# Spectra of 57 complex numbers stored without padding to 64, in a four-layer convolution kernel

## The chip, the cores and the metric

The kernel runs on one core of a Trainium2 chip. That core has a matrix engine (TensorE, PE in the profile), three engines for elementwise work and reductions (VectorE or DVE, ScalarE or ACT, GpSimd or POOL), a queue engine (SyncE or SP) and 16 DMA engines that move data between the chip's DRAM and the on-chip memory of 128 partitions. The metric is the device time of one execution in microseconds (us); each number is a median of runs.

## What is computed

The input x has shape 32 x 64 x 112 x 112, float32. Four residual layers follow each other, each on the group-normalized input (32 groups of two channels):

```
# layer 0: 3x3 convolution of the signs with ternary weights
x = x + conv(sign(gn(x)), round(tanh(w0))) * alpha
# layer 1: spectral mixing
x_ft = rfft2(gn(x), norm='ortho')                      # 112 x 57 complex
xt   = x_ft[:, :, :56, :57]                            # min(64, 112//2), min(64, 57)
out  = einsum('bchw,cohw->bohw', xt, complex(w1))      # w1: 64 x 64 x 64 x 64 x 2
x = x + irfft2(out placed in zeros, s=(112, 112))
# layer 2: 7x7 convolution with bias
x = x + conv(gn(x), w2) + bias
# layer 3: windowed linear attention, windows of 8 x 8
x = x + attention(gn(x))
```

What matters here is layer 1: per image and channel a spectrum of 56 x 57 complex numbers. A row of it, 57 complex numbers, is 114 floats, 456 B.

## The kernel before

There are three stages, each a function with a block per engine. Within a stage every engine runs its own program, written out by hand, and semaphores alone order them. Nothing is scheduled by a planner.

**Stage A, `local_conv_and_forward_dft`** runs over the 32 images. SyncE loads x into `xc` (two halves of 1568 KB). TensorE does the 3x3 convolution from signs, VectorE adds (L316) and writes `x1s`, GpSimd's queue stores it to the DRAM tensor x1 in two halves (`store_x1`, L236). SyncE loads x1 again with image rows in the partitions (`xh`, `turn`, L206), which waits for both halves of the store (L200). TensorE transforms along rows (L470) and along columns (L477); ScalarE puts the results into `freq` (L409), 28 rows per partition, and GpSimd's queue stores them to the DRAM tensor `xf` in two parts of 16 and 12 rows (`store_freq`, L246). GpSimd's queue has, per image, in this order: x1 half 0, xf part 0, x1 half 1, xf part 1.

**Stage B, `mix_frequencies`** runs over KP = 28 steps k, each with two frequency rows at a time. SyncE loads, per pair of steps, weights `wt` (two transfers of 4096 KB, L529) and for each step the spectra `xs` of all images (2048 KB, L537). There are two weight buffers and one `xs`. VectorE turns `xs` into `xt` (L611 to L613), TensorE multiplies (L638), ScalarE and VectorE copy the sums into `ys` (L600, L617), and GpSimd's queue stores them to the DRAM tensor `yf` in four transfers of 512 KB per step (L563). `load_x(k)` waits until step k - 1 was turned (L536).

**Stage C, `large_conv_and_attention`** first prepares weights and then runs over the images: it loads both halves of an image's mixed spectrum into `ys` (`load_ys`, L1000) and x1 into `xr` (L1003), transforms back in two products (L1110 with `ys` as the weights, L1127), and does layers 2 and 3. `ys` is cleared once at the start (L1723). The load of the next image's `ys` is issued when L1110 is done with this one's.

The row length in all transfers comes from one constant:

```
KW = W // 2 + 1        # 57
FR = 2 * KW            # 114 floats of a row that are used
FP = 128               # floats of a row that are stored
```

`freq` has FP floats per row, xf is (KP, P, B, FP), `xs` is [P, B, FP // 2, 2], stage B's `ys` is [P, C, FP // 2], yf is (B, 2, KH, C, FP // 2), and stage C's `ys` is [P, C, FP // 2]. The pads of `freq` and of both `ys` are set to zero once. In stage C only the first 57 of the 64 columns matter: `inv_w` is zero for the others.

Of the kernel before, what the change touches and what calls it, by code (L numbers as in the profile page):

```python
# [14 lines left out]
P = 128  # L15
C = 64
# [5 lines left out]
KH = H // 2  # L22
KW = W // 2 + 1
KP = KH // 2
FR = 2 * KW
FP = 128
ROWS = 4
CHUNKS = J // ROWS
N4 = ROWS * W
# [4 lines left out]
def above_zero(count):  # L34


    return not isinstance(count, int) or count > 0
# [47 lines left out]
def pairs(eng, images, step):  # L85


    if images > 2:
        step(0)
    if images > 4:  # L90
        with eng.Fori(1, images // 2 - 1) as t:
            step(t)
# [30 lines left out]
def local_conv_and_forward_dft(nc, B, x, weight, alpha, cst, x1, xf):  # L123

    with ExitStack() as ctx:
# [7 lines left out]
        yw = sb("yw", [P, 2, KH, C])  # L133
        freq = sb("freq", [P, KP, FP])
        wraw = sb("wraw", [C, C, 9])
# [362 lines left out]
def mix_frequencies(nc, B, weight, xf, yf):  # L498

    with ExitStack() as ctx:  # L500
        sb = lambda name, shape, dt=F32: ctx.enter_context(nc.sbuf_tensor("b_" + name, shape, dt))
        sem = lambda name: ctx.enter_context(nc.semaphore("b_" + name))
        ps = ctx.enter_context(nc.psum_tensor("b_ps", [P, 8, BANK], F32))
        wt = sb("wt", [P, 2, C, 2, FP // 2, 2])
        xs = sb("xs", [P, B, FP // 2, 2])
        xt = sb("xt", [P, 2, KW, 3, B])
        ys = sb("ys", [P, C, FP // 2])
        w_loaded = [sem("w_loaded0"), sem("w_loaded1")]
# [390 lines left out]
def large_conv_and_attention(nc, B, args, cst, x1, yf, out):  # L899

    with ExitStack() as keep:
        sb = lambda name, shape, dt=F32: keep.enter_context(nc.sbuf_tensor("c_" + name, shape, dt))
# [3 lines left out]
        inv_h = sb("inv_h", [P, 2, H])  # L906
# [15 lines left out]
        sem = lambda name: keep.enter_context(nc.semaphore("c_" + name))  # L922
        ps = keep.enter_context(nc.psum_tensor("c_ps", [P, 8, BANK], F32))
        xr = sb("xr", [P, 2, J, W])
        ys = sb("ys", [P, C, FP // 2])


        xp_all = sb("xp", [P, 2 * 9 * (RING + 3) * PW], F16)
# [35 lines left out]
        s = type("Semaphores", (), {n: sem(n) for n in names})  # L964
# [27 lines left out]
        @block.sync  # L992
        def _(sp):
            def load_ys(n):
                if above_zero(16 * n):
                    sp.wait_ge(s.c1_done, 16 * n)
                    sp.nop(nofuse=True)
                for r in range(2):
                    src = yf[bass.ds(n, 1), r].rearrange("b k o w -> (b k) o w")
                    sp.dma_start(ys[64 * r:64 * r + KH], src).then_inc(s.ys_in, 16)  # L1000

            def load_x1(n, odd, a):
                sp.dma_start(xr[:, odd, 8 * a:8 * a + 8],  # L1003
                             x1[bass.ds(n, 1)].rearrange("b hp c j w -> (b hp c) j w")[:, 8 * a:8 * a + 8]
                             ).then_inc((x1_in if a < A7 - 1 else x1_end)[odd], 16)

            def load_next(t, odd, a):
                p = (odd + a) % 2
                sp.wait_ge(out_done[p], (A7 * t + ((A7 * odd + a - p) // 2 + 1)) * 32)
                sp.nop(nofuse=True)  # L1010
                load_x1(2 * t + (2 + odd), odd, a)

            def store(t, odd, more):
                n = 2 * t + odd
                for a in range(A7):
                    sp.wait_ge(s.xo_done, n * A7 + (a + 1))
                    sp.nop(nofuse=True)
                    for hp in range(2):
                        dst = out[bass.ds(n, 1), :, 16 * a:16 * a + 16].rearrange(
                            "b c (j hp) w -> hp (b c) j w", hp=2)[hp]  # L1020
                        sp.dma_start(dst, xr[C * hp:C * hp + C, odd, 8 * a:8 * a + 8]).then_inc(out_done[(odd + a) % 2], 16)
                    if more and a:
                        load_next(t, odd, a - 1)
                if more:
                    load_next(t, odd, A7 - 1)

            sp.wait_ge(s.zeros, 1)
            load_ys(0)
            for a in range(A7):
                load_x1(0, 0, a)  # L1030
            load_ys(1)
            for a in range(A7):
                load_x1(1, 1, a)

            def step(t):
                for odd in range(2):
                    load_ys(2 * t + (2 + odd))
                    store(t, odd, True)

            pairs(sp, B, step)  # L1040
            store(B // 2 - 1, 0, False)
            store(B // 2 - 1, 1, False)
            for p in range(2):
                sp.wait_ge(out_done[p], B // 2 * (A7 * 32))

        @block.tensor
        def _(pe):
# [37 lines left out]
            def stats(count, which):  # L1085
                pe.wait_ge(s.stats_done, count + 1)
                if above_zero(count):
                    pe.wait_ge(s.rstd_done, count)
                pe.matmul(ps[:, STAT_BANK[which], 0:2], group[:], st[:], start=True, stop=True).then_inc(s.grouped, 1)

            def bring(n, odd):
                row = (n - 1) * A7
                if above_zero(row):
                    numerator(row - 1)
                pe.wait_ge(s.ys_in, 32 * (n + 1))
                if above_zero(n):
                    pe.wait_ge(s.t_taken, n * (A7 * NT))
                for g in range(16):
                    if above_zero(row):
                        if g == 8:  # L1100
                            turn_back(row - 1)
                        if g == 12:
                            give_back(row - 1)

                    if g >= 4:
                        pe.wait_ge(s.c1_taken, n * 16 + (g - 3))
                        pe.nop(nofuse=True)
                    for o in range(4 * g, 4 * g + 4):
                        for r in range(2):
                            ins = pe.matmul(ps[64 * r:64 * r + 64, CONV_BANKS[g % 4], H * (o % 4):H * (o % 4) + H],  # L1110
                                            ys[0:120, o], inv_h[0:120, r],
                                            start=(o % 4 == 0), stop=(o % 4 == 3), skip_group_check=True)
                    ins.then_inc(s.c1_done, 1)
                if above_zero(n):
                    if above_zero(row):
                        pe.wait_ge(s.qt_taken, row)
                    stats(2 * n - 1, 1)
                pe.wait_ge(s.c1_taken, n * 16 + 16)
                for g in range(CHUNKS):
                    if g >= 4:  # L1120
                        taken = [c for c in range(g - 3) if c not in COPIED]
                        pe.wait_ge(s.x2_done, n * (CHUNKS - len(COPIED)) + len(taken))
                        copied = g - 3 - len(taken)
                        if copied:
                            pe.wait_ge(s.x2_copied, n * len(COPIED) + copied)
                    for j in range(4 * g, 4 * g + 4):
                        ins = pe.matmul(ps[:, CONV_BANKS[g % 4], W * (j % 4):W * (j % 4) + W],  # L1127
                                        z[:, 2 * j:2 * j + 2].rearrange("p h c -> p (h c)"), inv_w[:],
                                        start=(j % 4 == 0), stop=(j % 4 == 3), skip_group_check=True)
                    ins.then_inc(s.c2_done, 1)  # L1130
                if above_zero(n):
                    project(row, 0)
                    if above_zero(row):
                        pe.wait_ge(s.o2_done, row)
                stats(2 * n, 0)
                if above_zero(n):
                    project(row, 1)
# [17 lines left out]
            def numerator(l):  # L1155
                pe.wait_ge(s.kvm_done, 2 * l + 2)
                pe.nop(nofuse=True)
                for q in range(Q7):
                    for w in range(2):
                        for r in range(2):  # L1160
                            rows = slice(C * r, C * r + C)
                            ins = pe.matmul(ps[TOK * w:TOK * w + TOK, 4 + r, HEADS * q:HEADS * q + HEADS],  # L1162
                                            qt[rows, P * q + TOK * w:P * q + TOK * w + TOK], kvm[rows, w, q],
                                            start=(q == 0), stop=(q == Q7 - 1), skip_group_check=True)
                ins.then_inc(s.num_done, 1)

            def turn_back(l):
                pe.wait_ge(s.att_done, l + 1)
                for q in range(Q7):
                    ins = pe.transpose(ps[:, 4 + q // 4, P * (q % 4):P * (q % 4) + P],  # L1170
                                       att[:, q].rearrange("p r d h -> p (r d h)"), ident[:])
                ins.then_inc(s.turned_back, 1)
# [676 lines left out]
```

## Time and profile before

| | us |
|---|---|
| median of 3 runs | 11730.43 |
| lowest and highest | 11728.45, 11733.97 |
| the profiled execution's own time | 11728.25 |
| its span, first to last instruction | 11726.6 |
| PE busy | 10203.8 |
| DVE busy | 7999.6 |
| ACT busy | 6054.5 |
| POOL busy | 4027.2 |

The profile is one execution of the program. For each engine it records when instructions start and how long they take, and which wait ended the idle time before them; for the DMA queues it records packets with their size and the time they took on a DMA engine. The queue called q1, hardware_dynamic, has what SyncE issues; q0, software_dynamic, has what GpSimd issues; q8 and q14 fetch instructions and tables. All queues share the same 16 DMA engines. "Share of 16 engines" is the sum of the packets' times over 16 times the stretch; it can be somewhat above 100% where packets overlap on an engine. Packets of 4 B are the semaphore updates of transfers; they count among those under 512 B. TensorE's granted clock is a share of full speed.

### The profile page before, as it was taken

Reading aid. Unit: us, or ns where it says so; the run is one execution under the profiler, and the core shown is the slowest. Engines: PE = TensorE matmul, PEld = TensorE weight load, DVE = VectorE, ACT = ScalarE, POOL = GpSimd, SP = SyncE. Lnnn points to the kernel's source line nnn. Section 1 sums busy time; section 2 is a strip of 40 time slices with the busy share of each in tenths; the row PEclk is TensorE's granted clock in tenths of the full one; section 3 lists DMA queues with packets and bytes.
Section 4 is the critical chain, followed back from the end, with each engine's and each line's share of the span. In section 5 each row is a group of like instructions: output and inputs, shape, how many; then the busy total and the mean of one; then the engine's idle time right before and its main releaser. Section 6 shows DMA issues by size and latency. Waiting matters only on the chain.

```text
span 11726.6 us, 292194 instructions
## 1 busy us (share of the span) xinstructions
PE 10203.8 (87%) x120871; PEld 9034.3 (77%) x120871; DVE 7999.6 (68%) x13647; ACT 6054.5 (52%) x7030; POOL 4027.2 (34%) x3437
## 2 busy tenths in 40 slices
PE   7999967774999998999999999999998999999996
PEld 5777767674888887888888888888887888888885
DVE  7777733335677777777777777777777777777775
ACT  4666631112555555555555555555555555555553
POOL 0000000003444444444444444444444444444442
PEclk9999987776999999999999999999999999999997
DMA  8999989982011111111111111111111111111100
GB/s 205 240 240 242 244 193 234 232 219 61 19 33 33 30 41 30 30 30 31 30 33 30 33 32 31 33 30 33 31 40 30 30 30 31 30 33 33 30 22 17
DMA packets 662368, 888.86 MB, mean 76 GB/s; under 512 B 479008, under 2 KB 594704, under 8 KB 637776
## 3 DMA queue, kind: packets, MB, share of 16 engines
q1 hardware_dynamic: 631120, 650.33, 25.0%
q0 software_dynamic: 29952, 220.22, 5.1%
q8 instruction: 939, 15.38, 0.6%
q14 instruction: 357, 2.92, 0.1%
HBM read 547.51 MB, written 322.96 MB: 74 GB/s over the span
## 4 chain that ended last, share of the span: by engine, by line
PE 38%; DVE 17%; issue 7%; ACT 7%; POOL 5%; DMA 1%; SPq 0%; DVEq 0%; POOLq 0%; ACTq 0%
PE c_ps L1078 23%; PE c_ps L1149 3%; POOL c_cube L1789 3%; PE c_ps L1227 2%; PE c_ps L1162 2%; PE c_ps L1214 2%; DVE c_v L1591 2%; ACT c_xp L1335 2%; DVE c_xp L1555 2%; DVE c_bn L1535 2%; DVE c_s L1654 2%; DVE c_xr L1573 2%; ACT c_sq L1398 1%; PE c_ps L1110 1%; DVE c_qt L1629 1%
## 5 line engine op out<-in xcount | busy, mean ns | idle before, releaser
L1078 PE MATMUL c_ps<-c_xp,c_wst 128*128 128x224 f16 x45696 | 4900.0, 265 | 154.8 <-DVE c_xp L1555 154.8
L1078 PEld LDWEIGHTS c_ps<-c_xp,c_wst 128*128 128x128 f16 x45696 | 4362.9, 98 | 626.8 <-issue 415.6
L1764 POOL TENSOR_TENSOR c_xr<-c_sm,c_xr 128x448 f32<-128x448 f32 x448 | 704.2, 1572 | 2221.8 <-DVE c_xr L1573 2221.8
L1789 POOL TENSOR_TENSOR c_cube<-c_sq,c_qk 128x896 f32<-128x896 f32 x448 | 928.4, 2094 | 1191.3 <-ACT c_sq L1389 1191.3
L1366 ACT ACTIVATE c_qt<-c_ps 128x896 f32<-128x896 f32 x224 | 205.9, 919 | 2040.5 <-PE c_ps L1170 2040.5
L638 PE MATMUL b_ps<-b_wt,b_xt 64*64 64x64 f32 x12768 | 730.0, 285 | 336.2 <-DVE b_xt L613 192.6
L1324 ACT ACTIVATE c_tn<-c_xr,c_nrm 64x448 f32<-64x448 f32 (+1 forms) x832 | 956.0, 1153 | 56.9 <-DVE c_xp L1555 27.0
L638 PEld LDWEIGHTS b_ps<-b_wt,b_xt 64*64 64x64 f32 x12768 | 711.7, 170 | 354.4 <-issue 354.0
L1149 PE MATMUL c_ps<-c_wqkv,c_xn 64*128 64x192 f32 x6272 | 790.3, 367 | 200.7 <-DVE c_v L1591 193.2
L1335 ACT ACTIVATE c_xp<-c_tn 128x1080 f16<-128x1080 f32 (+1 forms) x544 | 572.3, 1063 | 730.2 <-DVE c_tn L1548 726.4
L1555 DVE TENSOR_TENSOR c_xp<-c_tn,c_xp 128x1080 f16<-128x1080 f32 (+1 forms) x544 | 664.1, 1231 | 271.7 <-ACT c_xp L1335 270.7
L1149 PEld LDWEIGHTS c_ps<-c_wqkv,c_xn 64*128 64x128 f32 x6272 | 516.3, 195 | 384.4 <-DVE c_v L1591 287.2
L1768 POOL TENSOR_TENSOR c_xr<-c_bs,c_xr 128x448 f32<-128x448 f32 x448 | 759.2, 1695 | 64.5 <-POOL c_xr L1764 0.4
L316 DVE SCALAR_TENSOR_TENSOR a_x1s<-a_ps,a_alph,a_xc 64x448 f32<-64x448 f32 x896 | 612.3, 683 | 212.2 <-PE a_ps L451 200.3
L1587 DVE TENSOR_TENSOR c_qk<-c_ps,c_bqk 128x512 f32<-128x512 f32 (+1 forms) x896 | 553.6, 618 | 287.6 <-PE c_ps L1149 285.5
L1654 DVE TENSOR_REDUCE c_s<-c_sq 128x28 f32<-128x1792 f32 x224 | 452.4, 2020 | 400.9 <-ACT c_sq L1398 400.9
L1345 ACT ACTIVATE c_xn<-c_xr,c_nrm 64x448 f32<-64x448 f32 x896 | 675.7, 754 | 26.5 <-DVE c_nrm L1468 17.5
L451 PE MATMUL a_ps<-a_signs,a_wst 128*128 128x448 bf16 x2688 | 614.8, 367 | 62.2 <-DVE a_x1s L316 47.8
L1750 POOL TENSOR_TENSOR c_tn<-c_tn 128x224 f32<-128x224 f32 (+1 forms) x480 | 372.8, 777 | 822.4 <-ACT c_tn L1324 814.7
L600 ACT ACTIVATE b_ys<-b_ps 64x512 f32<-64x512 f32 x224 | 194.1, 953 | 872.2 <-DMA yf<-b_ys 536.8
L1776 POOL TENSOR_TENSOR c_xr<-c_kvm,c_xr 128x896 f32<-128x896 f32 x224 | 469.8, 2097 | 464.0 <-ACT c_kvm L1375 464.0
L398 ACT ACTIVATE a_yw<-a_ps 112x448 f32<-112x448 f32 x512 | 450.1, 945 | 331.4 <-PE a_ps L470 331.3
(160 smaller groups left out, 17319.0 us busy)
## 6 DMA issues: line engine op xcount, KB each, us to landing
b_wt<-in_L_conv_weight SPq DMA_DIRECT2D x28, 4096.0 KB, 42.7
a_xc<-in_x SPq DMA_DIRECT2D x64, 1568.0 KB, 21.6
x<-a_x1s POOLq DMA_DIRECT2D x64, 1568.0 KB, 11.6
a_xh<-x SPq DMA_DIRECT2D x64, 1568.0 KB
c_xr<-x SPq DMA_DIRECT2D x224, 448.0 KB, 4.2
out<-c_xr SPq DMA_DIRECT2D x448, 224.0 KB, 3.1
b_xs<-xf SPq DMA_DIRECT2D x28, 2048.0 KB, 24.1
yf<-b_ys POOLq DMA_DIRECT2D x112, 512.0 KB, 9.8
```

Source lines behind the costliest of these rows:

```text
L451: ins = pe.matmul(ps[:, c % 3, 0:N4], wst[:, pr, kx].rearrange("p q o -> p (q o)"), signs[:, odd, ROWS * c + pr:ROWS * c + pr + ROWS, kx:k ...
L638: ins = pe.matmul(ps[C * half:C * half + 2 * B, 4 * half + g % 4, at:at + C], xt[rows, u, f, 1 - r:3 - r].rearrange("p r b -> p (r b)"), w ...
L1078: ins = pe.matmul(sums(c, p), wst[:, ws, pr, FIRST_TAP[p] + k].rearrange("p q o -> p (q o)"), xp[:, xs, PLANE[kind] + f, row:row + CROWS, ...
L1149: ins = pe.matmul(ps[:, 2 + r, 3 * C * (q % 2):3 * C * (q % 2) + 3 * C], xn[rows, 2 * q:2 * q + 2].rearrange("p w t -> p (w t)"), wqkv[row ...
L1324: ins = act.activation(pad_put(k)[to, :, a - lo:b - lo], pad_get(odd)[of, :, a - first:b - first], ACT.Identity, scale=nrm[of, 0, 0:1], bi ...
L1335: ins = act.activation(xp[:, 0, :, at:at + rows].rearrange("p k j w -> p k (j w)"), tn[:, k % 2, 0:9, 0:rows].rearrange("p k j w -> p k (j ...
L1345: ins = act.activation(xn[C * wr:C * wr + C].rearrange("p w (j hp x) -> p hp j w x", hp=2, x=WS)[:, hp], xr[C * hp:C * hp + C, odd, 8 * a ...
L1555: ins = dve.tensor_tensor(xp[:, 1, :, at:at + rows].rearrange("p k j w -> p k (j w)"), tn[:, k % 2, 0:9, 0:rows].rearrange("p k j w -> p k ...
L1654: dve.tensor_reduce(sums(s6), squares(sq), AX.X, ALU.add).then_inc(s.s6_done, 1)
L1764: pool.tensor_tensor(here, apart(sm[:, half]).unsqueeze(1).to_broadcast([P, 2, CROWS, QW]), here, ALU.add).then_inc(s.added, 1)
L1768: ins = pool.tensor_tensor(here, bs[:, 0:2].rearrange("p f (j i) -> p f j i", j=CROWS), here, ALU.add)
L1789: pool.tensor_tensor(cube[:, :, k].rearrange("p q r c -> p r q c"), sq[:, :, :, k], qk[:, :, :, k], ALU.mult).then_inc(done, 1)
```

## The change

FP becomes FR, 114 floats, so a row is 456 B instead of 512 B in `freq`, xf, `xs`, both `ys` and yf. Three places that used FP for something else follow. The weights' tile `wt` in stage B, whose rows of 64 come from the input as they are, now names 64. In stage C `ys` gets one more channel of room, is loaded into the first 64, and the weights of L1110 (L1111 in the new file) are 64 columns from a flat view that start at 57 times the channel's number, so the last seven columns are those of the next channel (or the cleared room behind the last). They meet zeros of `inv_w` in the next product.

```diff
-FP = 128
+FP = FR
@@ mix_frequencies
-        wt = sb("wt", [P, 2, C, 2, FP // 2, 2])
+        wt = sb("wt", [P, 2, C, 2, 64, 2])
@@ large_conv_and_attention
-        ys = sb("ys", [P, C, FP // 2])
+        ys = sb("ys", [P, C + 1, KW])
+        ys_flat = ys[:].rearrange("p o w -> p (o w)")
@@ load_ys
-                    sp.dma_start(ys[64 * r:64 * r + KH], src).then_inc(s.ys_in, 16)
+                    sp.dma_start(ys[64 * r:64 * r + KH, 0:C], src).then_inc(s.ys_in, 16)
@@ bring
-                                            ys[0:120, o], inv_h[0:120, r],
+                                            ys_flat[0:120, KW * o:KW * o + 64], inv_h[0:120, r],
```

The built programs have the same instructions in the same order on all five engines. What differs is shapes: the xf store has rows of 114 elements for 128, the `xs` load, the yf stores and the `ys` load have 3648 elements per partition for 4096, and the two memsets and the write into `freq` are shorter or contiguous. An image's part of xf is 128 x 28 rows, now 14592 B apart instead of 16384 B; each of them begins at the image's number times 456 B. The `xs` load reads 14592 B per partition, the yf stores write as much per (image, row).

## Rows read from the trace of the kernel before

**Rows 1.** Busy time by stretch: engines in us (instructions), TensorE's granted clock, DMA share, GB/s.

```profile
core 0: us, PE busy (x) PEld busy (x) DVE busy (x) ACT busy (x) POOL busy (x), PEclk, DMA share, GB/s
0.00:1602.40 1602.40, 1399.35 (x10505) 1139.48 (x10505) 1218.52 (x2185) 972.71 (x930) 121.02 (x136) 0.96 0.95 230
400.00:1200.00 800.00, 727.09 (x5506) 597.73 (x5506) 634.55 (x1146) 509.60 (x488) 54.46 (x66) 0.97 1.00 242
1602.40:2683.10 1080.70, 729.98 (x12768) 711.71 (x12768) 331.60 (x308) 194.06 (x224) 58.32 (x113) 0.75 0.89 219
1700.00:2500.00 800.00, 583.85 (x10207) 569.19 (x10209) 267.24 (x248) 152.05 (x176) 45.05 (x92) 0.77 0.91 231
...
2820.00:11726.60 8906.60, 8059.47 (x97472) 7169.97 (x97472) 6361.89 (x10976) 4869.51 (x5857) 3774.54 (x3136) 0.95 0.12 31
```

**Rows 2.** Waits from 400 to 1200 us: who for whom, total us, times, longest.

```profile
DVE a_bnx L294 <- DMA a_xc<-in_x: 34.8, 16, 4.3
PE a_ps L470 <- DMA a_xh<-x: 33.8, 16, 3.1
...
SPq L200 <- DMA x<-a_x1s: 408.3, 17, 24.9
```

**Rows 3.** Timeline of SyncE's and GpSimd's transfer issues: start us, us, what.

```profile
805.23 9.79 SPq L206 DMA_DIRECT2D a_xh<-x  x2
...
852.13 7.12 SPq L206 DMA_DIRECT2D a_xh<-x  x2
...
826.47 1.17 POOL L246 DMA_DIRECT2D xf<-a_freq  x1 [18.60 <-ACT a_freq L409]
829.61 0.54 POOL L236 DMA_DIRECT2D x<-a_x1s  x1 [1.98 <-DVE a_x1s L316]
```

**Rows 4.** The same timeline in the second stage, SyncE, VectorE, GpSimd.

```profile
2121.55 47.96 SPq L537 DMA_DIRECT2D b_xs<-xf  x2
2170.21 26.79 SPq L529 DMA_DIRECT2D b_wt<-in_L_conv_weight  x2
...
2243.84 24.00 SPq L529 DMA_DIRECT2D b_wt<-in_L_conv_weight  x2
...
2163.96 1.73 DVE L611 TENSOR_SCALAR b_xt<-b_xs 128x1824 f32<-128x1824 f32 x1 [16.63 <-DMA b_xs<-xf]
...
2171.68 2.25 POOL L563 DMA_DIRECT2D yf<-b_ys  x4 [45.34 <-DVE b_ys L617]
```

**Rows 5.** Queues' packets, MB, share of 16 engines: 1700:2500; 2171.5:2175; 2161:2170.

```profile
q0 software_dynamic: 4414, 48.22, 15.6%
...
q1 hardware_dynamic: 79, 1.29, 98.4%
...
q1 hardware_dynamic: 7, 0.07, 1.7%
```

**Rows 6.** SyncE's waits in the whole second stage.

```profile
SPq L536 <- DVE b_xt L613: 306.5, 23, 26.3
```

**Rows 7.** Transfers from 851 to 852 us, only the spectrum's store.

```profile
DMA packets 88, 0.32 MB, mean 324 GB/s; under 512 B 9, under 2 KB 9, under 8 KB 88
...
q0 software_dynamic: 88, 0.32, 85.7%
```

**Rows 8.** Transfers of 448 B rows: 4528:4531 (out stores), then 815:817 (xh load).

```profile
q1 hardware_dynamic: 664, 0.29, 44.1%
...
q1 hardware_dynamic: 133, 0.06, 10.4%
```

**Rows 9.** Line L1110's loads, products and waits; then SyncE's issue of its load.

```profile
L1110 PEld LDWEIGHTS c_ps<-c_inv_h,c_ys x8192: 132/137/232, 2820.0 to 11234.7; 120*64 120x64 f32 x200
L1110 PE MATMUL c_ps<-c_inv_h,c_ys x8192: 258/259/450, 2820.0 to 11234.8; 120*64 120x112 f32 x200
...
  DMA c_ys<-yf: 60.3, 1
...
2807.77 0.75 SPq L1000 DMA_DIRECT2D c_ys<-yf  x2
```

## The prediction, made before the changed kernel ran

> **What bounds the kernel now.** I read the stages first [rows 1]: each row gives a stretch, its busy time by engine, TensorE's granted clock, and the busy share of the 16 DMA engines. The first stage (local convolution and forward transform) takes 1602 us, the second (mixing of frequencies) 1081 us, the third the last 8907 us. In the middle of the first stage the DMA engines are 100% busy and TensorE 727 of 800 us; in the middle of the second DMA is 91% busy and TensorE 584 of 800; in the third DMA is 12% busy. The change takes bytes away and no arithmetic. So it can pay in the first two stages only, and the reader has to find out there, transfer by transfer, whether a DMA engine's time is the time of the stage.
>
> First stage: the row of SyncE's waits says that each image's reload of x1 with rows first (xh) waits 24 us for the store of x1 (408.3 us in 17 waits), and TensorE and VectorE wait for xh and for the next image (33.8 and 34.8 us in 800) [rows 2]. In time: xh is issued at 805.2, next at 852.1; between them GpSimd's queue holds the first part of the spectrum (826.5) and behind it the second half of x1 (829.6) [rows 3]. So the loop of an image, 46.9 us, is: xh, the next x, the spectrum's first part, x1, xh again, all on full DMA engines. A spectrum store that takes longer delays x1 and with it the loop.
>
> Second stage: SyncE puts weights and spectra on one queue, two b_xs loads and two b_wt loads per pair of iterations. The pair that begins at 2170.2 begins the moment the three copies to b_xt that start at 2164.0 are done; b_xs had been waited for [rows 4]. Between 2161 and 2170 DMA moved next to nothing (1.7%), in the rest of the pair it is full [rows 5]. SyncE waits 306.5 us in this stage, in 23 waits, for b_xt [rows 6]. The loop of a pair is therefore b_xs, 8 MB of weights, b_xs, and some 9 us of landing and copying in which nothing is loaded. The two yf stores per pair are issued within it (one at 2171.7) and share the same engines. TensorE is not the bound, so this is DMA time nearly one for one.
>
> **The change, part by part.** The order and number of instructions on all engines stay; only shapes change. I sum against the profiled execution, 11728.25 us (span 11726.6), 2 us below the median of 11730.43.
>
> *b_xs loads.* 28 of them, each 128 rows of 16384 B, now 14592 B (57/64, 10.9% less), contiguous on both sides as before. In a pure stretch 79 of these packets took 98.4% of 16 engines for 3.5 us: 697 ns each [rows 5]. Per load 128 x 697 / 16 = 5.6 us of all engines, and 10.9% of it is 0.61 us.
>
> *yf stores.* Per iteration 4 stores of 32 rows of 16384 B, now 14592 B. The software queue's row has 48.22 MB, that is 2943 packets of 16384 B, in 15.6% of 16 x 800 us: 678 ns each [rows 5], 5.4 us per iteration, 0.59 us less. Together 1.20 us x 28 iterations = 34 us. Lower bound: the fixed 9 us per pair don't shrink and I assumed that all of a store lies in the loop; were only b_xs in it, 17 us. Upper bound: none of it hidden and the packets that were slowed by sharing shrink more, 40 us. I take 34.
>
> *Copies around them.* The reading step of the b_xt copies goes from 512 to 456 B, the writing step of the b_ys copies from 256 to 228 B. No row shows such a step. Both run beside the weights' transfer except for the b_xt copies, which sit in the loop [rows 4]. The b_xt group is three instructions between 2164.0 and 2169, so each is about 1.7 us for 1824 elements per partition, about one element per 0.94 ns, and the b_xt side already writes contiguously: 0, within -10 to +10 us over the stage.
>
> *xf stores.* This is the term that decides. Per image 128 partitions x 28 rows; a row was 512 B and is 456 B, in xf at a distance of 14592 B instead of 16384. The row of a pure stretch shows 88 packets, 9 of them under 512 B (the semaphore writes), and 0.32 MB: 79 packets of 4096 B, 8 rows each, at 0.857 x 16 us / 79 = 174 ns [rows 7]. So an image's store is 448 packets, 448 x 174 / 16 = 4.9 us of all 16 engines, of a loop of 46.9 us. If the queue goes on putting 8 rows into a packet, 10.9% less would be 0.53 us; the cost of a row that isn't bytes doesn't shrink, which would leave about 0. I take half, 0.27 us, over the 30 images that have the loop: 8 us less, bounds 16 and 0. If rows go singly instead, the nearest rows are the 448 B packets of the other queue: 25.0 ns each when undisturbed (133 packets in 10.4% of 16 x 2 us), and 31.9 ns for the out stores of the third stage (664 packets in 44.1% of 16 x 3 us), against 174 / 8 = 21.8 ns now [rows 8]. That is 3584 x 25 to 32 / 16 = 5.6 to 7.2 us per image, 0.7 to 2.3 us more, 22 to 68 us in 30 images. I give the first case the better chance, because the present packets are cut by bytes and not by partition: 12 rows of a partition make no whole number of packets of 8, and still 4096 B is what the row shows.
>
> The Trainium skill bears on this in "DMA: Bandwidth & Descriptors", section "SWDGE vs HWDGE vs iDMA": packets of the software queue are preferably up to 4096 B and at most 64 descriptors. By it 8 rows of 456 B still make a packet, and the sum stays as I take it; this trace agrees with it for 512 B rows.
>
> *Third stage.* c_ys is loaded once per image, 2 x 56 rows, 10.9% less. TensorE waited for it once, at the start, 60.3 us, and never again [rows 9]; the load is issued at 2807.8 and TensorE's first product is at 2820.0 [rows 9], of which some 10 us are transfer: 1.1 us less. For the other 31 images the load has a whole image's time, in a stage with 12% DMA [rows 1]: 0. The weights are now 64 columns that start at multiples of 228 B and run 7 columns into the next channel's row (multiplied by zeros of inv_w later). Their load is 137 ns beside products of 259 ns [rows 9], so it could grow by 120 ns before it showed: 0. If that cover were gone, 10 ns more on each of 8192 loads would be 82 us.
>
> Sum: 34 + 8 + 1 = 43 us less: 11728.25 - 43 = 11685, on the median 11687 us.
>
> **The rivals.**
> 1. *Rows go out singly, at today's cost for short rows.* For it: the other queue sends every 448 B row as a packet of its own [rows 8]. Against it: the 4096 B packets [rows 7]. At 28 ns, between the two rows, an image's spectrum takes 6.3 us, 1.4 more, 42 in 30 images: 34 + 1 - 42 = -7, about 11737 on the median. No measurable change, and a trade inside the kernel: the second stage gains what the first loses.
> 2. *Rows below 512 B that begin at odd places cost double (the other side).* 456 is no multiple of 64, so 28 of 32 images begin their rows inside a 64 B piece, and rows 456 B long are written in part at both ends. No row of this trace shows such a write: the 448 B rows begin at multiples of 64. If a row takes 52 ns instead of 26, an image's spectrum takes 11.6 us, 6.8 more, and since the store sits ahead of x1 in a full queue it all shows: 203 us in 30 images, minus 35, about +168, 11898 us. It outweighs the gain from 35 / 30 = 1.2 us more per image, that is from 27 ns a row. A milder form, 35 ns, gives 3 us more per image, +54, 11784.
> 3. *The second stage is not a loop of DMA time.* If TensorE, whose idle time there also has other causes, or the copies end the pair, the transfers are hidden already. For it: DMA is 91%, not 100%. Against: the pair starts when b_xt is copied, and DMA stands still just then. Then only 8 + 1 us are left, 11721.
>
> For rival 2 the same page of the Trainium skill, section "Specifications", says that a transfer needs 512 B or more for line rate and that below this the engine reads, modifies and writes. The 448 B stores of this trace at 31.9 ns speak against a doubling, though they are aligned to 64 B.
>
> **How the numbers follow.** Forecast (8 rows to a packet) 0.45; rival 1 0.30; rival 2 in one of its forms 0.14; rival 3 0.11. The predicted time is that of the first, 11687, its own range 11672 to 11707 (copies and bounds of the terms). The range for 8 in 10 must take in rival 1, 11717 to 11763 by its bounds of 22 to 68 us, and rival 3; it leaves out rival 2 and the ends: 11670 to 11768. A measurement of this kernel tells about 0.2%, 23 us, from no change. Faster by more than that: nearly all of the forecast, a little of rival 1: 0.45. Slower by more: rival 2 and the dear end of rival 1: 0.21. Within: 0.34.
>
> **What would show it.** In the profile after: the software queue's packets in the first stage (3648 B or 456 B, and the time of each); the distance between two xh issues (46.9 us now; 46.6, 48.3 or above 50); the distance between two pairs of b_wt issues (73.6 us now, 2170.2 to 2243.8 [rows 4]; 2.4 less); the end of the first stage (1602) and of the second (1081 long); DMA standing still in each pair as before. A start of the third stage at other than 137 us after the second, or a load of c_ys weights over 137 ns, would make the third stage's zero wrong. The forecast is wrong if xf rows cost over 27 ns.

## The result: 1.3% slower, all of it in the first stage

| | us | against before |
|---|---|---|
| before, median of 4 | 11729.93 (11728.45 to 11733.97) | |
| with the change, median of 4 | 11882.61 (11855.62 to 11897.19) | 1.0126, 95% interval 1.011 to 1.0142 |
| forecast | 11687 | |

The stretches of the three stages in the profile after, with the middle of the first (columns as in [rows 1]); the first stage ends where SyncE issues the first load of weights for the second:

```profile
core 0: us, PE busy (x) PEld busy (x) DVE busy (x) ACT busy (x) POOL busy (x), PEclk, DMA share, GB/s
0.00:1793.50 1793.50, 1409.38 (x10505) 1145.33 (x10505) 1217.65 (x2185) 969.85 (x930) 121.27 (x136) 0.91 0.95 202
400.00:1200.00 800.00, 650.23 (x4904) 534.96 (x4903) 564.50 (x1019) 453.04 (x434) 49.70 (x60) 0.92 1.00 212
1793.50:2829.30 1035.80, 729.66 (x12768) 711.49 (x12768) 357.27 (x308) 207.11 (x224) 58.27 (x114) 0.77 0.88 216
...
2963.50:11879.30 8915.80, 8081.97 (x97472) 7186.85 (x97472) 6363.36 (x10976) 4870.84 (x5857) 3775.20 (x3136) 0.95 0.12 30
```

The first stage takes 1793.5 us instead of 1602.4 [rows 1], 191 more. The second takes 1035.8 instead of 1080.7, 45 less. In the middle of the first stage DMA is as full as before (100%), but moves 212 GB/s instead of 242, and TensorE works 650 of 800 us instead of 727. The third stage, from its first product on, takes 8916 instead of 8907; below it turns out that this is no effect of the change.

The waits of the same middle (who for whom, total us, times, longest) answer to [rows 2]:

```profile
PE a_ps L470 <- DMA a_xh<-x: 107.6, 10, 31.6
...
DVE a_bnx L294 <- DMA a_xc<-in_x: 42.4, 13, 9.3
...
SPq L200 <- DMA x<-a_x1s: 303.4, 14, 30.1
```

TensorE now waits 107.6 us for xh instead of 33.8, once for 31.6. SyncE's waits for the store of x1 are up to 30 us long.

What the two queues did in the same 800 us (packets, MB, share of 16 engines):

```profile
q1 hardware_dynamic: 110340, 96.34, 65.4%
q0 software_dynamic: 11120, 72.99, 34.4%
```

The corresponding rows of before:

```profile
q1 hardware_dynamic: 122827, 108.19, 71.0%
q0 software_dynamic: 13049, 85.76, 29.1%
```

An image's x1 and spectrum were 5.05 MB on q0, so that is 17.0 images at 13.7 us of all engines each; now they are 4.85 MB, 15.1 images at 18.3 us. So an image costs 4.6 us more on the queue that carries xf. q1, which carries nothing changed in this stage, went from 71.0% / 17.0 to 65.4% / 15.1 images, 33.4 to 34.7 us: 1.3 more. Together 5.9 us an image, 177 us in 30 images, of the 191.

The packet records of the whole stage part the 4.6 us by size. The spectrum's own packets took 5.9 us of all engines per image before and 8.9 after, 3.0 more; a row cost 26.1 ns in the mean and now costs 39.7. The other 1.6 us are the packets of x1, whose shape did not change: 492 ns each before, 589 after.

Four microseconds of the store of one image's spectrum in the profile after:

```profile
DMA packets 75, 0.41 MB, mean 103 GB/s; under 512 B 6, under 2 KB 12, under 8 KB 68
...
q0 software_dynamic: 67, 0.24, 75.0%
q1 hardware_dynamic: 8, 0.18, 31.0%
```

The engines are full, 75 + 31%, and move 103 GB/s. This is one of the worst stretches: 61 data packets (67 less 6 semaphore writes), most of them 4104 B and a few a leftover of two rows, take 0.75 x 16 x 4 / 61 = 787 ns each, against 174 ns where before was undisturbed [rows 7]. In the mean of the whole stage a packet of 4104 B took 352 ns, one of 4096 B before 209.

The second stage, two issues of weights eleven pairs apart, first after, then the matching ones of before:

```profile
1923.51 22.58 SPq L529 DMA_DIRECT2D b_wt<-in_L_conv_weight  x2
...
2688.34 22.66 SPq L529 DMA_DIRECT2D b_wt<-in_L_conv_weight  x2
```

```profile
1735.40 24.94 SPq L529 DMA_DIRECT2D b_wt<-in_L_conv_weight  x2
...
2531.38 26.80 SPq L529 DMA_DIRECT2D b_wt<-in_L_conv_weight  x2
```

A pair takes (2688.3 - 1923.5) / 11 = 69.5 us instead of 72.4.

### The profile page after: what moved, and what is told of

The parts are those of the page before. It is cut to its first block, busy times and chain, and to the rows that moved or that the text cites. A ratio compares the mean times of both kernels' runs of the same rounds, so it can differ in the third digit from the quotient of the medians.

```text
span 11879.3 us, 292194 instructions
## 1 busy us (share of the span) xinstructions
PE 10236.1 (86%) x120871; PEld 9056.8 (76%) x120871; DVE 8025.9 (68%) x13647; ACT 6066.0 (51%) x7030; POOL 4027.6 (34%) x3437
## 3 DMA queue, kind: packets, MB, share of 16 engines
q0 software_dynamic: 28928, 207.37, 6.1%
## 4 chain that ended last, share of the span: by engine, by line
PE 38%; DVE 17%; issue 7%; ACT 7%; POOL 5%; DMA 1%; DVEq 0%; SPq 0%; POOLq 0%; ACTq 0%
PE c_ps L1079 23%; PE c_ps L1150 3%; POOL c_cube L1790 3%; PE c_ps L1228 3%; PE c_ps L1163 2%; PE c_ps L1215 2%; DVE c_v L1592 2%; ACT c_xp L1336 2%; DVE c_xp L1556 2%; DVE c_bn L1536 2%; DVE c_s L1655 2%; DVE c_xr L1574 2%; ACT c_sq L1399 1%; DVE c_qt L1630 1%; DVE c_qk L1602 1%
## 5 line engine op out<-in xcount | busy, mean ns | idle before, releaser
L470 PE MATMUL a_ps<-a_fh,a_xh 112*112 112x112 f32 x4096 | 474.8, 269 | 221.2 <-DMA a_xh<-x 220.5
L470 PEld LDWEIGHTS a_ps<-a_fh,a_xh 112*112 112x112 f32 x4096 | 468.9, 185 | 255.3 <-issue 195.5
```

The lines of the kernel that those rows point to most:

```text
L470: ins = pe.matmul(ps[0:W, 4 + g % 3, H * c:H * c + H], xh[0:H, odd, 4 * g + c], fh[:], start=(c == 0), stop=(c == 3), skip_group_check=True)
```

## The experiments

My theory after the result (P below) was that a row of xf is dear when it ends or begins inside a small piece of memory. The rivals were that rows shorter than 512 B are dear (L below), that the new distance between the partitions' rows is (D below), and that the store's place in GpSimd's queue makes the loss.

Each row of the table is one kernel. "Ends" is how many ends of a row of xf, in the mean over the images, lie inside a piece of 32 B; "distance" is from one partition's rows to the next's. It also sets how far apart the rows of one partition lie, 128 distances, since xf has the row number outside the partition; no run changes one without the other. First and second stage are read from SyncE's issues as above, in us.

| kernel | row of xf | distance | ends | stage 1 | stage 2 |
|---|---|---|---|---|---|
| before | 512 | 16384 | 0 | 1602.4 | 1080.7 |
| e6, before again | 512 | 16384 | 0 | 1599.2 | 1080.6 |
| e2, only yf packed | 512 | 16384 | 0 | 1602.1 | 1049.5 |
| e5 | 448 | 14336 | 0 | 1599.9 | 1027.2 |
| e1 | 480 | 15360 | 0 | 1608.8 | 1041.7 |
| e14 | 480 | 16384 | 0 | 1606.5 | 1042.4 |
| e7 | 464 | 14848 | 1 | 1618.5 | 1042.9 |
| e13 | 456 | 14848 | 1.5 | 1658.6 | 1039.8 |
| e10 | 472 | 15104 | 1.5 | 1684.7 | 1035.8 |
| **the change** | 456 | 14592 | 1.5 | 1793.5 | 1035.8 |
| e4 | 456 every 512 | 16384 | 1 | 1899.8 | 1137.3 |
| e3 | 456 | 16384 | 1.5 | 1952.6 | 1034.8 |
| e12 | 464 | 16384 | 1 | 1959.2 | 1046.7 |
| e8 | 512, 8 B off | 16384 | 2 | 2033.5 | 1047.6 |
| e9 | 512, 16 B off | 16384 | 2 | 2112.5 | 1054.8 |

The whole times of single executions follow the stages; where a ratio was timed it is given. Each stage time is that of one execution. The same kernel gave 1602.4 and 1599.2 (before and e6) and 1559.5 and 1570.8 (e15 and e16, below), and four executions of the change lie between 11855.62 and 11897.19 us. So differences of some 10 us, and of some 40 us between kernels with odd ends, say nothing.

**e1, rows of 480 B.** `xf`, `freq` and `xs` get rows of FX floats, the rest stays packed:

```diff
+FX = 120
-        freq = sb("freq", [P, KP, FP])
+        freq = sb("freq", [P, KP, FX])
-        xs = sb("xs", [P, B, FP // 2, 2])
+        xs = sb("xs", [P, B, FX // 2, 2])
-    xf = nc.dram_tensor("xf", (KP, P, B, FP), f32, kind="Internal").ap()
+    xf = nc.dram_tensor("xf", (KP, P, B, FX), f32, kind="Internal").ap()
```

> The changed kernel, but a row of the first spectrum (freq, xf, xs) is 120 floats, 480 B, so every row in xf begins and ends on a multiple of 32 B; the second spectrum (yf) stays packed at 57. Theory P (pieces of 32 B written in part are dear: in the changed kernel each 456 B row has one or two): the first stage goes back to about 1602 us or a little less, from 1793.5, the second is about 1045, the whole about 11690 to 11705. Theory L (any row below 512 B is dear): the first stage stays near 1790, the whole near 11880. Theory D (the distance of rows in DRAM, 14592 B instead of 16384 B, spreads badly): with 15360 B no firm number, but a first stage between 1602 and 1793.

Measured: 11703.77 us, ratio 0.9978 (0.9968 to 0.9987). SyncE's first issue for the second and for the third stage:

```profile
1608.81 16.53 SPq L530 DMA_DIRECT2D b_wt<-in_L_conv_weight  x2
...
2650.46 0.34 SPq L750 DMA_DIRECT2D c_ident<-cst_ident  x1
```

The first stage is back at 1609. Rows shorter than 512 B are not dear as such: theory L falls.

**e2, rows of 512 B, yf packed.** As e1 with `FX = 128`.

> The changed kernel with the first spectrum's rows of 512 B again; only the second spectrum (yf and its loads) is packed. All three theories: first stage 1602 us as before. My sum for the second stage's stores: 0.59 us x 28 = 17 us less of the second stage's 1081, and 1 us at the start of the third: 11711. If the stores were hidden there: 11728.

Measured: 11699.92 us, ratio 0.9978 (0.9968 to 0.9987).

```profile
1602.11 16.81 SPq L530 DMA_DIRECT2D b_wt<-in_L_conv_weight  x2
...
2651.62 0.34 SPq L750 DMA_DIRECT2D c_ident<-cst_ident  x1
```

The first stage is before's. The second, 1049.5 us, is 31 us shorter where I expected 17.

**e3, 456 B rows 16384 B apart per partition.**

```diff
-    xf = nc.dram_tensor("xf", (KP, P, B, FP), f32, kind="Internal").ap()
+    xf = nc.dram_tensor("xf", (KP, P, B * 128), f32, kind="Internal").ap()
-                dst = xf[4 * lo:4 * hi, :, bass.ds(n, 1)].rearrange("k p b f -> p k (b f)")
+                dst = xf[4 * lo:4 * hi, :, bass.ds(n * FP, FP)].rearrange("k p f -> p k f")
```

> The changed kernel with rows of 456 B next to each other as there, but each partition's 32 rows begin at a multiple of 16384 B in xf, as before the change. Theory P and theory L: first stage stays at 1780 to 1800 us. Theory D: first stage back to about 1602 us.

(The load of xs in SyncE's program follows the new shape.) Measured: 12035.89 us in one execution.

```profile
1952.56 16.31 SPq L529 DMA_DIRECT2D b_wt<-in_L_conv_weight  x2
...
2987.32 0.34 SPq L749 DMA_DIRECT2D c_ident<-cst_ident  x1
```

Theory D falls in the form that I gave it, and the 1780 to 1800 us of theories P and L missed as well: the distance counts, the other way round. At before's distance the same rows cost 350 us instead of 191.

**e4, 456 B rows that begin at multiples of 512 B** (from the kernel before).

```diff
-                dst = xf[4 * lo:4 * hi, :, bass.ds(n, 1)].rearrange("k p b f -> p k (b f)")
-                pool.dma_start(dst, freq[:, 4 * lo:4 * hi]).then_inc(freq_out[part], 16)
+                dst = xf[4 * lo:4 * hi, :, bass.ds(n, 1), 0:FR].rearrange("k p b f -> p k (b f)")
+                pool.dma_start(dst, freq[:, 4 * lo:4 * hi, 0:FR]).then_inc(freq_out[part], 16)
```

> The kernel before, but of each 512 B row only the 456 B in use are stored, each row beginning at a multiple of 512 B; the loads of xs take the same 456 B rows singly (4096 rows a load instead of 128), so the second stage is expected longer and tells nothing of the store. Theory P: every row now has exactly one end inside a 32 B piece (456 is 8 more than a multiple of 32), the images that had one in the changed kernel took 300 ns a packet against 389 for those with two and 210 before, so the first stage lies at about half of the loss, 1680 to 1720 us. Theory L: near 1790. A theory that only an odd beginning costs: 1602.

Measured: 12092.02 us in one execution, first stage 1899.8. A beginning at a round place does not help; the single odd end of a row is enough for 297 us at this distance. The rows of `freq` on the chip lie 512 B apart here, as in e8 and e9 below, so odd places on the chip are not needed for the loss; e13 below reads `freq` as the changed kernel does and loses only 56 us. My "half of the loss" assumed the changed kernel's distance and missed. (Its second stage, 1137 us, shows what loading `xs` in rows of 456 B would cost: 57 us.)

**e5, rows of 448 B**, the last complex number of each left out.

> The changed kernel with rows of 448 B in xf and xs (7 pieces of 64 B), by leaving out the last of the 57 complex numbers of each row in the first spectrum; the store has the same number of rows as in all others. Theory P (pieces of 32 B written in part): first stage at most 1602 us, since no row has a partial piece and bytes are 12.5% fewer; packets of 10 rows, 4480 B. Theory L (rows below 512 B): near 1790. If pieces of 64 B also count for something, the packets here are cheaper per row than those of 480 B rows were (about 259 ns for 9 rows at the median): about 180 to 190 ns for 10 rows.

Measured: 11670.57 us in one execution, first stage 1599.9: the shortest rows cost nothing.

**e6, before once more.**

> The kernel before, word for word, for a second profile on this chip. The third stage, from its first product to the end, took 8907 us in the first profile of before and 8913 to 8918 in all five others, one of them (456 B rows at multiples of 512 B) with a third stage like that of before. If that is a matter of the run and not of the packed ys, it is here also above 8907; if packed ys costs it, 8907. Second stage: 1081 us if the 31 us that packing yf alone saved are real, and not a difference between runs.

Measured: 11725.08 us; stages 1599.2 and 1080.6. So the 31 us that e2 saved in the second stage are real. The third stage from its first product took 8908.0 us here and in e5, which has packed ys, and 8918 in e4, whose third stage is before's. Over all 19 profiles it lies between 8903 and 8925 us. Packing is not what moves the third stage by 10 us; what does, no run here tells.

**e7, rows of 464 B** (`FX = 116`).

> The changed kernel with rows of 464 B: each row has exactly one end inside a 32 B piece, where 456 B rows have one in half of the images and two in the other half, 1.5 in the mean. Theory P, cost in proportion to partial pieces: two thirds of the loss of 191 us, a first stage of about 1730 us, between 1700 and 1760. If it were the odd 8 B steps as such: 1602 to 1610. Theory L: near 1790.

Measured: 11723.07 us in one execution, first stage 1618.5:

```profile
1618.52 16.46 SPq L530 DMA_DIRECT2D b_wt<-in_L_conv_weight  x2
```

The proportion to the number of ends failed: one end per row cost 16 us, not 127. A row of 464 B took 28.6 ns in the mean, one of 480 B in e1 28.3 ns, so at this distance the odd end itself cost next to nothing.

**e8 and e9, whole 512 B rows, all of xf shifted by 8 or 16 B.**

```diff
+def shifted(xf, B):
+    return xf[SHIFT:SHIFT + KP * P * B * 128].rearrange("(k p b f) -> k p b f", k=KP, p=P, b=B)
-    xf = nc.dram_tensor("xf", (KP, P, B, FP), f32, kind="Internal").ap()
+    xf = nc.dram_tensor("xf", (KP * P * B * 128 + 64,), f32, kind="Internal").ap()
```

with `SHIFT` 2 and 4 floats.

> Rows of 512 B again (only yf packed, as in the run with 1602 us for the first stage), but all of xf begins 8 B later, so every row of 512 B has both ends inside a 32 B piece. Theory L: 1602 us. Theory P: at least the 350 us that 456 B rows (1.5 partial pieces) lost at the same distance of 16384 B, 1950 to 2100 us for the first stage.

> As the run with 512 B rows shifted by 8 B (first stage 2034 us), but shifted by 16 B: both ends of every row still lie inside a 32 B piece, but no piece of 16 B is written in part. The 464 B rows, one such end each, cost only 16 us. Theory P16 (what is dear is a piece of 16 B written in part): first stage 1600 to 1625 us. Theory P32 (any piece of 32 B in part): above 1900 us.

Measured: 12138.65 and 12221.84 us. SyncE's issues in e8, then in e9:

```profile
2033.48 16.56 SPq L536 DMA_DIRECT2D b_wt<-in_L_conv_weight  x2
...
3081.07 0.34 SPq L756 DMA_DIRECT2D c_ident<-cst_ident  x1
```

```profile
2112.50 16.47 SPq L536 DMA_DIRECT2D b_wt<-in_L_conv_weight  x2
...
3167.26 0.34 SPq L756 DMA_DIRECT2D c_ident<-cst_ident  x1
```

This is the plainest proof: rows as long as before, as many, as far apart and in the same packets cost 431 us more for a shift of 8 B. The shift by 16 B costs 510, so theory P16 (formed after e7) falls too, and pieces of 32 B stay. Whether 16 B off is dearer than 8 B, two single executions don't tell.

**e10, rows of 472 B** (`FX = 118`).

> The changed kernel with rows of 472 B, an odd number of 8 B as 456 B is, 15104 B between a partition's rows. Theory P16: as dear as 456 B, a first stage of 1770 to 1850 us, though 464 B and 480 B on either side took 1619 and 1609. If 456 B were dear for another reason (its packets of 9 rows, or the distance of 14592 B): 1605 to 1625.

Measured: 11777.07 us, first stage 1684.7. Dear, but by 82 us and not by 170 to 250: with as many odd ends as 456 B rows have, at another distance. That left the distance open.

**e12, e13, e14: row and distance changed separately**, as e3, with `(row, distance)` = (464, 16384), (456, 14848), (480, 16384).

> Rows of 464 B next to each other (one end of each inside a 32 B piece), a partition's 32 rows 16384 B apart instead of 14848 B. Theory PD (a piece of 32 B written in part costs, and the distance decides how much): first stage 1850 to 1950 us, like the 1900 of 456 B rows with one such end at that distance, against 1618.5 at 14848 B. If 464 B rows are cheap by themselves: 1605 to 1625.

> Rows of 456 B, 14848 B between a partition's rows instead of 14592 B, the distance at which 464 B rows cost 16 us. Theory PD: much of the 191 us gone, a first stage of 1620 to 1700 us. If the row length decides and not the distance: 1770 to 1820 us.

> Control: rows of 480 B (whole pieces of 32 B, every row with one half of a 64 B piece) at the worst distance, 16384 B. Theory PD with pieces of 32 B: 1600 to 1620 us. If pieces of 64 B written in part cost too, this distance shows it: above 1800.

Measured: 12045.62, 11755.49 and 11706.18 us. SyncE's first issues for the second stage in e12, e13 and e14:

```profile
1959.23 16.57 SPq L531 DMA_DIRECT2D b_wt<-in_L_conv_weight  x2
```

```profile
1658.60 16.44 SPq L531 DMA_DIRECT2D b_wt<-in_L_conv_weight  x2
```

```profile
1606.53 16.45 SPq L531 DMA_DIRECT2D b_wt<-in_L_conv_weight  x2
```

The same 464 B rows cost 16 us at 14848 B and 357 at 16384. The same 456 B rows cost 56 us at 14848, 191 at 14592 and 350 at 16384. Rows of whole 32 B pieces cost 4 us at the distance that is worst for all others, and each of them has a half piece of 64 B. So both are needed, an end inside a piece of 32 B and an unlucky distance. e12 lies 9 us above the range that I gave for it, e13 and e14 lie within theirs.

**e11, the order of GpSimd's queue.** In the changed kernel, x1 half 1 ahead of the spectrum's part 0:

```diff
-                if rest:
-                    store_freq(n, 0)
                 if conv:
                     store_x1(n + 2, 1)
+                if rest:
+                    store_freq(n, 0)
```

> The changed kernel (456 B rows), with GpSimd's queue in another order: an image's x1 half 1 is stored before the two parts of the spectrum instead of between them, so xh no longer waits behind the dear store of part 0. If the loss of 191 us came from the place in the queue alone: a first stage of 1610 to 1660 us. If it is time of the DMA engines, which are full (my account): 1770 to 1820, since the same packets run in the same loop.

Measured: 11973.05 us, first stage 1888.8. The place in the queue alone was not the cause: with x1 ahead of the dear store the stage became 95 us longer. The packets of 4104 B took 509 ns in the mean instead of 352, those of x1 526 instead of 589. That both parts of the spectrum now meet the load of xh would explain it, but is not shown. Neither forecast held.

**e15 and e16, the same order with 512 B rows** (e2 with e11's edit), **e17 with 480 B rows.**

> The kernel with 512 B rows and only yf packed (first stage 1602 us), in the order of e11: x1 half 1 ahead of both parts of the spectrum. e11 lost 95 us more than the changed kernel. If the order itself costs that: about 1700. If the order only brings the dear packets together with others that they slow down: 1595 to 1615.

> The kernel of e15 again, timed: 512 B rows in the first spectrum, packed rows in the second, x1 half 1 ahead of both parts of the spectrum in GpSimd's queue. One execution took 11663.7 us beside 11717.4 of before: a ratio of 0.995, 55 to 70 us less than before.

> The same order with 480 B rows in the first spectrum, whole pieces of 32 B. In e1 these rows cost 6 us in the first stage and saved 8 in the second against 512 B rows: within 5 us of e16. If x1's store now shares more with the spectrum's dearer rows (28.6 against 26 ns), up to 15 us more.

Measured: e15 11663.72 us in one execution; e16 11668.28 us, ratio 0.995 (0.9934 to 0.9967); e17 11669.56 us, ratio 0.9956 (0.9943 to 0.9969). The first stage takes 1559.5 us in e15, 1570.8 in e16, 1578.2 in e17. Two rows of e15, the stretch from 400 to 1200 us and SyncE's wait for x1's store:

```profile
400.00:1200.00 800.00, 741.45 (x5728) 610.69 (x5726) 657.68 (x1188) 524.56 (x508) 57.01 (x69) 0.99 1.01 252
...
SPq L201 <- DMA x<-a_x1s: 325.4, 18, 19.6
```

DMA moves 252 GB/s instead of 242, SyncE waits 18 us for x1 instead of 24, and TensorE works 741 of 800 us. I had not expected this gain: with cheap rows the order saves some 31 to 43 us (1602.1 of e2 less 1570.8 or 1559.5), with dear ones it loses 95. The kernels of e16 and e17 beat the kernel before by 0.5% and 0.4%, and the changed one with it.

## Why the prediction was wrong, step by step

**What bounds the kernel: right.** DMA time is the first stage's time: 5.9 us more of it per image made 191 us in the stage. The pair loop of the second stage was right too.

**b_xs and yf: right in kind, the terms mis-sized.** 34 us forecast, 45 measured. The 45 lie above my upper bound of 40. yf alone (e2) gave 31 us, for which I had 17; b_xs then gave 1049.5 - 1035.8 = 14, for which I had 17, with the slower copies of the next paragraph in it. For yf it was too little to count a store's bytes alone. By the packet records of the second stage its packets went from 708 to 616 ns, 21 us of all engines over the stage, the packets of the loads took 5 us less, and the time without DMA shrank by about as much again. Why that time shrank is not shown.

**The copies: not zero.** VectorE's groups of the second stage (busy us, mean ns) in the profile after:

```profile
L617 DVE COPY b_ys<-b_ps 64x512 f32<-64x512 f32 x196 | 199.1, 1094 | 470.0 <-DMA yf<-b_ys 365.5 <-PE b_ps L638 103.5
L611 DVE TENSOR_SCALAR b_xt<-b_xs 128x1824 f32<-128x1824 f32 x28 | 53.4, 1908 | 209.1 <-DMA b_xs<-xf 199.9 <-PE b_ps L638 8.7
```

The corresponding rows of before:

```profile
L617 DVE COPY b_ys<-b_ps 64x512 f32<-64x512 f32 x196 | 185.6, 1018 | 483.4 <-DMA yf<-b_ys 379.0 <-PE b_ps L638 103.5
L611 DVE TENSOR_SCALAR b_xt<-b_xs 128x1824 f32<-128x1824 f32 x28 | 49.2, 1758 | 261.7 <-DMA b_xs<-xf 261.3
```

The copies to b_xt became 150 ns longer, 0.45 us per turn, some 6 us over the 14 that sit in the loop: within the bounds that I gave.

**xf: the step that failed.** It is the term that I called deciding: "8 us less, bounds 16 and 0". The runs showed 191 us more for the stage in its place. I expected the queue to go on filling packets by bytes. It did: q0 has 28928 packets in the whole run instead of 29952, 1024 fewer, 32 an image, which is what packets of 9 rows (4104 B) instead of 8 give; I had taken 8, to stay within 4096 B. It also fills them across partitions, as I had read: the leftovers are packets of 912 and 2736 B, two and six rows. But I concluded from the packet to its price. "10.9% less would be 0.53 us ... about 0" as bounds of the case left out that the price of a row depends on where it ends, although my rival 2 said just that. A row went from 26.1 to 39.7 ns, far over the 27 ns that I had named as the sign of being wrong. The 174 ns a packet that I started from were those of an undisturbed microsecond as well; the mean was 209 ns, 5.9 us an image and not 4.9.

Rival 2 had the right kind of cause, and its sum came close: 203 us forecast for the stage, 191 measured; 11898 us in all, 11883 measured. That closeness is in good part luck. It put the whole 6.8 us an image on the spectrum's rows, at a doubled 52 ns that no row supported. They took only 3.0 us more, and the rest of the loss is the slowing of other packets, which the rival did not have. It had no effect of the distance either, which moves the same rows between 56 and 350 us. I gave it 0.14, because rows of 448 B were cheap [rows 8]. That was the error in weighing: 448 is a multiple of 32 (and of 64), so those rows could not say anything about ends inside a piece. I even wrote that no row of this trace showed such a write, and then let the nearest row decide. Rival 2's own unit, 64 B, was wrong as well: e1 and e14 have half pieces of 64 B in every row and lose 4 to 6 us. So was its condition "below 512 B", as e8 shows.

**The rule of the page, as rival 2 cited it.** The runs differ from the Trainium skill ("DMA: Bandwidth & Descriptors", "Specifications"), by which the engine reads, modifies and writes below 512 B: 448 and 480 B rows cost nothing to speak of (e5, e1; 26.1 and 28.3 ns a row against 26.1 at 512 B), and 512 B rows cost 431 us when they began 8 B late (e8). The measurement decides: what counts here is whole pieces of 32 B, not 512 B.

**Rivals 1 and 3** are out: rows did not go singly, and the second stage did gain.

**Third stage: right.** From the issue of c_ys to the first product it takes 1.4 us less (2952.7 to 2963.5 against 2807.8 to 2820.0 [rows 9]) for 1.1 forecast. The loads of the weights from odd places take as long as before (shortest, mean and longest in ns):

```profile
L1111 PEld LDWEIGHTS c_ps<-c_inv_h,c_ys x8192: 132/137/230, 2963.4 to 11387.8; 120*64 120x64 f32 x200
```

**What stays open.** Why an odd end costs more at 16384 B than at 14592, and there more than at 14848, was not found; the runs only show that it does, and that other queues' packets slow down with it. That the memory reads a piece, changes and rewrites it would fit, but no run here shows such a read. The distance was tried with odd ends at four values only, and always together with the 128 times larger one between the rows of a partition, so either of the two may be what counts.

## What to carry to other kernels

Cut padding in DRAM to a multiple of 32 B per written row, not to the last byte: with 456 B rows the packing turned into a loss, with 480 B rows it did not. But those rows gained nothing over 512 B rows either: 7 us more in the first stage and 8 less in the second, both near the spread between executions. The 0.9978 of e1, some 23 us, about half of the forecast gain, is the one of yf, which e2 has alone. Long contiguous transfers are worth packing where the loop is full of DMA. Those of yf here, 14592 B, still begin and end on multiples of 32 B; no run shows a long transfer with odd ends. Before judging a new row length by a similar one in the trace, ask which property of it the similar one shares, and give the unseen property its own chance.

## What the runs showed of the hardware that I had not expected

- DRAM rows that begin or end inside a piece of 32 B took 39.7 ns in the mean of the stage instead of 26.1 (456 B at 14592), and 62.2 ns for 512 B rows begun 8 B late (e8). Other packets slow down with them: those of x1 took 589 ns instead of 492, and in one of the worst stretches full DMA engines moved 103 GB/s in all.
- The same odd rows cost 16 or 357 us in the first stage by their spacing in DRAM alone (464 B, e7 and e12).
- VectorE's first operation on the spectra, 1824 elements, took 1758 ns with a reading step of 512 B, and 1908, 2059, 1830 and 1899 ns with 456, 464, 472 and 480 B.
- Moving one store ahead of another in a full queue gained 0.3% of the kernel with cheap rows and lost 0.8% with dear ones (e11, one execution).
